# Splitting the first loads of a float32 feature network by partitions over two DMA queues, with seven fewer warm-up matmuls

## The reference

```python
w = jnp.einsum('bpf,mf->bpm', features, W_ft) + b_ft
accumulator = stm * w
l1_x = jnp.clip(accumulator, 0.0, 1.0).reshape(features.shape[0], -1)
l2_x = jnp.clip(l1_x @ W1.T + b1, 0.0, 1.0)
return l2_x @ W2.T + b2
```

## Time and profile before

| | us |
|---|---|
| median of 3 runs | 399.14 |
| lowest and highest of them | 398.35, 399.34 |
| the profiled execution, its own time | 398.15 |
| its span, first to last instruction | 396.4 |
| TensorE matmul busy | 392.8 (99%) |
| VectorE busy | 346.9 (88%) |
| ScalarE busy | 197.6 (50%) |
| HBM read | 96.87 MB, 244 GB/s over the span |

### The profile page before, as it was taken

The page is one execution under the profiler, slowest core; times in us unless marked ns, Lnnn a source line. Parts: engine busy times, 40 slices in busy tenths (PEclk is TensorE's granted clock), DMA queues, the critical chain, the costliest instruction groups (busy, mean ns, idle before and its releaser), DMA issues.

```text
span 396.4 us, 4869 instructions
## 1 busy us (share of the span) xinstructions
PE 392.8 (99%) x1862; PEld 323.7 (82%) x1862; DVE 346.9 (88%) x347; ACT 197.6 (50%) x207; POOL 14.7 (4%) x34
## 2 busy tenths in 40 slices
PE   8999999999999999999999999999999999999997
PEld 6888888888888888888888888888788888878886
DVE  3999999999999999999997789999787754999624
ACT  5565556633484434444334864344433447863500
POOL 0000034041000000000000000000000000000000
PEclk9999999999999999999999999999999999999999
DMA  8999979989976677666607689887667778774000
GB/s 271 394 398 400 383 247 362 342 256 230 327 255 233 237 254 263 243 220 235 233 0 256 225 317 397 327 308 236 203 233 257 241 217 247 245 246 132 0 2 3
DMA packets 30775, 97.85 MB, mean 247 GB/s; under 512 B 4024, under 2 KB 10176, under 8 KB 25312
## 3 DMA queue, kind: packets, MB, share of 16 engines
q1 hardware_dynamic: 29392, 95.18, 69.0%
q0 software_dynamic: 1072, 2.10, 1.7%
q10 hardware_dynamic: 288, 0.26, 0.2%
HBM read 96.87 MB, written 0.00 MB: 244 GB/s over the span
## 4 chain that ended last, share of the span: by engine, by line
PE 99%; DVE 0%; issue 0%; DVEq 0%
PE sums L595 94%; PE sums L672 3%; PE sums L711 1%; PE sums L698 1%; PE sums L688 0%; PE sums L706 0%; DVE res L528 0%; DVE hid L522 0%; DVE idle L531 0%; DVEq L527 0%
## 5 line engine op out<-in xcount | busy, mean ns | idle before, releaser
L595 PE MATMUL sums<-x_hi,w_hi 128*128 128x512 f32 x544 | 167.2, 391 | 0.0
L595 PE MATMUL sums<-x_hi,w_lo 128*128 128x512 f32 x544 | 166.5, 389 | 0.0
L595 PEld LDWEIGHTS sums<-x_hi,w_hi 128*128 128x128 f32 x544 | 102.1, 188 | 21.9 <-issue 0.7
L595 PEld LDWEIGHTS sums<-x_hi,w_lo 128*128 128x128 f32 x544 | 102.4, 188 | 21.3
L595 PE MATMUL sums<-x_lo_home,w_hi 128*128 128x512 f32 x384 | 118.4, 389 | 0.0
L355 ACT ACTIVATE x_hi<-xs 128x2048 fp32r<-128x2048 f32 x58 | 110.7, 1908 | 2.2 <-DVE xs L490 1.8
L350 ACT ACTIVATE w_hi<-ws 128x512 fp32r<-128x512 f32 x58 | 36.9, 636 | 147.1 <-PE sums L595 139.0
L499 DVE TENSOR_TENSOR x_lo_home<-xs,x_hi 128x2048 fp32r<-128x2048 f32 x40 | 91.3, 2283 | 12.3 <-ACT x_hi L355 12.3
L595 PEld LDWEIGHTS sums<-x_lo_home,w_hi 128*128 128x128 f32 x384 | 72.1, 188 | 15.0
L483 DVE TENSOR_TENSOR xs<-xs 128x2048 f32<-128x2048 f32 x20 | 45.6, 2281 | 0.7 <-DMA xs<-x_p 0.7
L496 DVE TENSOR_TENSOR w_lo<-ws,w_hi 128x512 fp32r<-128x512 f32 x58 | 39.6, 683 | 6.2 <-ACT w_hi L350 6.1
(11 more groups left out here) (72 smaller groups left out, 199.5 us busy)
## 6 DMA issues: line engine op xcount, KB each, us to landing
xs<-x_p SPq DMA_DIRECT2D x40, 1024.0 KB, 5.7
xs<-x_p SPq DMA_DIRECT2D x56, 512.0 KB, 6.4
ws<-w_p SPq DMA_DIRECT2D x56, 256.0 KB, 3.5
ws<-w_p SPq DMA_DIRECT2D x44, 128.0 KB, 4.7
open_x<-x_p SPq DMA_DIRECT2D x3, 512.0 KB, 6.2
xr_raw<-x_rest POOLq DMA_DIRECT2D x1, 1024.0 KB, 8.5
stm_all<-stm SPq DMA_DIRECT2D x1, 1024.0 KB, 7.6
open_x<-x_p SPq DMA_DIRECT2D x2, 256.0 KB, 4.3
```

The costliest lines, as they stand in the source:

```text
L595: return nc.tensor.matmul(sums[:, bank, :], w[:, m * P:(m + 1) * P], x[:, c * BANK:(c + 1) * BANK], start=start, stop=stop, skip_group_che ...
```

## The change

A new input, `head`, is laid out on the host: for each of 128 partitions the first 512 columns of X of step 0 and the 256 columns of W of step 0 side by side, 768 float32, 3 KB a partition. It is loaded by two transfers, partitions 0 to 63 on SyncE's queue and 64 to 127 on ScalarE's. The other 512 columns of X of step 0, and X of step 1, are split by partitions over the two queues in the same way. W of step 1 moves from ScalarE's queue to SyncE's, between them. The rounding of the first piece is shared: ScalarE rounds columns 0 to 319 of X (`SHARE`), VectorE rounds W and columns 320 to 511 (`share_hi`). X of step 1 is rounded in two pieces instead of one. Warm-ups go from 22 to 15. Everything from step 2 on is as it was. `highs_before` counts one rounding less than `halves_before`, since W's is no longer ScalarE's.

```diff
+SHARE = 320
-WARM_UP = 22
+WARM_UP = 15
...
+        head_in = sb("head_in", [P, BANK + MH], at=c_at + 4 * (STAGED * COLS - BANK))
...
         def pieces(g, pos):
-            if (g, pos) == (0, 0) or (g < STAGED and pos == 1):
+            if pos == 0 and g < 2 or pos == 1 and g < STAGED:
                 return (0, BANK), (BANK, COLS)
...
+        def open_b11(g, a, b):
+            if g:
+                return open_x[:, STAGED - 1 - g, a:b]
+            return head_in[:, a:b] if b <= BANK else open_x[:, STAGED - 1, a - BANK:b - BANK]
+
+        def open_a11(g):
+            return open_w[:, g, :] if g else head_in[:, BANK:]
...
         def _(sp):
-            sp.dma_start(open_x[:, 0, 0:BANK], x_p[0, :, 0, 0:BANK]).then_inc(open_x_loaded[0], 16)
-            sp.dma_start(open_x[:, 0, BANK:COLS], x_p[0, :, 0, BANK:COLS]).then_inc(open_x_loaded[STAGED], 16)
+            sp.dma_start(head_in[0:P // 2, :], head[0:P // 2, :]).then_inc(head_in_loaded[0], 16)
+            sp.dma_start(open_x[0:P // 2, STAGED - 1, 0:BANK], x_p[0, 0:P // 2, 0, BANK:COLS])\
+                .then_inc(open_x_loaded[0], 16)
+            sp.dma_start(open_w[:, 1, :], w_p[1, :, 0, :]).then_inc(open_w_loaded[1], 16)
...
-                    sp.dma_start(open_x[:, g, :], x_p[g, :, 0, :]).then_inc(open_x_loaded[g], 16)
+                    rows = P // 2 if g == 1 else P
+                    sp.dma_start(open_x[0:rows, STAGED - 1 - g, :], x_p[g, 0:rows, 0, :])\
+                        .then_inc(open_x_loaded[g], 16)
...
-                if pos == 0 and g < STAGED:
+                if (g, pos) == (0, 0):
+                    for j in range(2):
+                        sc.wait_ge(head_in_loaded[j], 16)
+                    nc.scalar.activation(x_hi[:, 0, 0, 0:SHARE], open_b11(0, 0, SHARE), ACT.Copy).then_inc(open_hi, 1)
+                    sc.wait_ge(open_x_loaded[0], 16)
+                    sc.wait_ge(open_x_late[0], 16)
+                    nc.scalar.activation(x_hi[:, 0, 0, BANK:COLS], open_b11(0, BANK, COLS), ACT.Copy)\
+                        .then_inc(open_hi, 1)
+                elif pos == 0 and g < STAGED:
...
-            for g in range(2):
-                sc.dma_start(open_w[:, g, :], w_p[g, :, 0, :]).then_inc(open_w_loaded[g], 16)
+            sc.dma_start(head_in[P // 2:P, :], head[P // 2:P, :]).then_inc(head_in_loaded[1], 16)
+            sc.dma_start(open_x[P // 2:P, STAGED - 1, 0:BANK], x_p[0, P // 2:P, 0, BANK:COLS])\
+                .then_inc(open_x_late[0], 16)
+            sc.dma_start(open_x[P // 2:P, STAGED - 2, :], x_p[1, P // 2:P, 0, :]).then_inc(open_x_late[1], 16)
...
+            for j in range(2):
+                dve.wait_ge(head_in_loaded[j], 16)
+            nc.vector.tensor_copy(w_hi[:, 0, 0, :], open_a11(0)).then_inc(share_hi, 1)
+            nc.vector.tensor_copy(x_hi[:, 0, 0, SHARE:BANK], open_b11(0, SHARE, BANK)).then_inc(share_hi, 1)
...
             def open_products(n, g, pos):
                 before = halves_before(n)
+                rounded = highs_before(n)
...
+                if n == 0:
+                    pe.wait_ge(share_hi, 2)
                 for i, cs in enumerate(groups):
-                    pe.wait_ge(open_hi, before + 2 + i)
+                    pe.wait_ge(open_hi, rounded + 2 + i)
...
+        "head": np.concatenate([x_p[0, :, 0, :BANK], w_p[0, :, 0, :]], axis=1),
```

More of the change, by code:

```diff
@@ L53, in pass_of, with feature_net @@
     return f, g - f * K_PAIRS
-def feature_net(nc, x_p, w_p, x_rest, w_rest, stm, b_ft, w1_t, b1, w2_t, b2, out):
+def feature_net(nc, head, x_p, w_p, x_rest, w_rest, stm, b_ft, w1_t, b1, w2_t, b2, out):
     L1 = w1_t.shape[2]
@@ L132, in feature_net @@
         open_w_loaded = [sem(f"open_w_loaded{j}") for j in range(STAGED)]
-        open_x_loaded = [sem(f"open_x_loaded{j}") for j in range(STAGED + 1)]
+        head_in_loaded = [sem(f"head_in_loaded{j}") for j in range(2)]
+        open_x_late = [sem(f"open_x_late{j}") for j in range(2)]
+        open_x_loaded = [sem(f"open_x_loaded{j}") for j in range(STAGED)]
         open_hi = sem("open_hi")
         open_lo = sem("open_lo")
+        share_hi = sem("share_hi")
         a_done = sem("a_done")
@@ L230, in halves_before, with highs_before @@
             return sum(1 + len(pieces(*half)) for half in OPEN_HALVES[:n])
+        def open_b11(g, a, b):
[4 more added lines that the diff above has]
+            return open_w[:, g, :] if g else head_in[:, BANK:]
+        def highs_before(n):
+            return halves_before(n) - 1
         def x_sums(g):
@@ L317, in open_half @@
                     sc.wait_ge(step_done if pos else a_done, g - HI + 1)
-                if pos == 0 and g < STAGED:
+                if (g, pos) == (0, 0):
[7 more added lines that the diff above has]
+                elif pos == 0 and g < STAGED:
                     sc.wait_ge(open_w_loaded[g], 16)
-                    nc.scalar.activation(w_hi[:, g % HI, 0, :], open_w[:, g, :], ACT.Copy).then_inc(open_hi, 1)
+                    nc.scalar.activation(w_hi[:, g % HI, 0, :], open_a11(g), ACT.Copy).then_inc(open_hi, 1)
                     sc.wait_ge(open_x_loaded[g], 16)
[L322 to L325, removed]
+                    if g == 1:
+                        sc.wait_ge(open_x_late[1], 16)
+                    for a, b in pieces(g, 0):
+                        nc.scalar.activation(x_hi[:, g % HI, 0, a:b], open_b11(g, a, b), ACT.Copy).then_inc(open_hi, 1)
                 elif pos == 0:
@@ L432, in open_low @@
             def open_low(n, g, pos):
-                before = halves_before(n)
+                before = highs_before(n)
                 if pos == 0 and g < STAGED:
-                    w_src, x_src = open_w[:, g, :], open_x[:, g, :]
-                elif pos == 0:
-                    w_src, x_src = ws[:, raw_w(g), :], xs[:, raw_x(g), :]
-                else:
-                    w_src, x_src = ws[:, raw_w(g) + 1, :], xs[:, TST + g, :]
-                dve.wait_ge(open_hi, before + 1)
+                    w_src = open_a11(g)
+                else:
+                    w_src = ws[:, raw_w(g) + pos, :]
+                if n == 0:
+                    dve.wait_ge(share_hi, 1)
+                else:
+                    dve.wait_ge(open_hi, before + 1)
                 nc.vector.tensor_tensor(w_lo[:, slot(g), pos, :], w_src, w_hi[:, g % HI, pos, :].bitcast(F32),
                                         ALU.subtract).then_inc(open_lo, 1)
+                if n == 0:
+                    dve.wait_ge(share_hi, 2)
                 for i, (a, b) in enumerate(pieces(g, pos)):
                     dve.wait_ge(open_hi, before + 2 + i)
-                    nc.vector.tensor_tensor(low_x(g)[:, pos, a:b], x_src[:, a:b],
+                    if pos == 0 and g < STAGED:
+                        x_src = open_b11(g, a, b)
+                    else:
+                        x_src = xs[:, TST + g if pos else raw_x(g), a:b]
+                    nc.vector.tensor_tensor(low_x(g)[:, pos, a:b], x_src,
                                             x_hi[:, g % HI, pos, a:b].bitcast(F32), ALU.subtract)\
@@ L454, in sums_of @@
                 if f == 0:
-                    if staged:
+                    if 0 < g < STAGED:
                         dve.wait_ge(open_w_loaded[g], 16)
@@ L462, in sums_of @@
                         dve.wait_ge(open_x_loaded[g], 16)
-                        if g == 0:
-                            dve.wait_ge(open_x_loaded[STAGED], 16)
+                        if g < 2:
+                            dve.wait_ge(open_x_late[g], 16)
                     else:
                         dve.wait_ge(x_loaded[n], x_count(g))
-                    b11 = open_x[:, g, :] if staged else xs[:, j, :]
                     for a, b in pieces(g, 1):
-                        nc.vector.tensor_tensor(xs[:, TST + k, a:b], xs[:, TST + k, a:b], b11[:, a:b],
-                                                ALU.subtract).then_inc(x_sum, 1)
+                        b11 = open_b11(g, a, b) if staged else xs[:, j, a:b]
+                        nc.vector.tensor_tensor(xs[:, TST + k, a:b], xs[:, TST + k, a:b], b11, ALU.subtract).then_inc(x_sum, 1)
                     if k >= LATE_S2:
```

## The result

| | before | after |
|---|---|---|
| median of 16 runs each | 398.35 | 400.17 |
| lowest and highest | 397.59, 399.34 | 398.74, 402.32 |
| the profiled execution, its own time | 398.15 | 401.79 |
| its span | 396.4 | 399.9 |

The ratio of after to before is 1.0051, with a 95% interval of 1.0036 to 1.0066: slower by 0.5%, more than the 0.3% that the prediction set as its bound. The forecast was 399.3 with no measurable change; its range held the result. The medians of this table differ by 1.82, and of the four cases the first rival (the clock rises later), at +1.7, comes nearest to that. The profiled execution lies 1.6 us above its kernel's median, so it shows the mechanism at more than its median size.

A forecast was written before the change was run, and what follows sets the result against it. The prediction took TensorE's first-product start and product pace as the bound. The later start gave +0.2, other terms +0 and +0; added to 399.14, the profiled execution corrected to the median, this made 399.3, range 398.2 to 401.5.

The forecast's parts named there:

- the first rival: TensorE idle ahead of the first product makes its clock rise later: +1.0 to +2.5, middle +1.7, 400.8; chance 0.38.
- The likeliest case: First product near 5.9 and the clock's rise as before: 398.9 to 399.7, all within 0.3%; chance 0.40.
- What bounds the kernel: TensorE's unbroken matmuls: only the first real product's start and the products' pace can move the end.
- The landing of the head: Opening transfer of X's first piece and W of step 0: lands at 4.1, between 3.4 and 4.84.
- The table load behind the landing: ScalarE's 1.28 us ACT_TABLE_LOAD waits for the head; first product at 5.94 instead of 5.61, worth +0.2 us.
- VectorE's casts: Rounding of W and X's 192 columns on VectorE: done by 4.9, hidden under the table load.
- I take the rise as unmoved, at 7.05: +0.: Seven warm-ups less leave TensorE idle about 1.6 us before the products, yet its clock rises at 7.05: +0.
- The bytes come when they came: SyncE's transfers issue one slot, some 0.45 us, later, but the DMA backlog keeps landings unchanged: price 0.
- All three covers hold: X's second piece, X of step 1 and VectorE's later remainders stay in time for TensorE: price of each 0.
- The table load is not in the way: Rival at the start: VectorE's casts decide, first product at 4.25 to 4.95; 398.4 to 398.8; chance 0.10.
- the halves land no earlier: Rival at the head: landing stays at 4.84, start at 6.68; +0.6, 399.7, more if the clock rises later; chance 0.12.

The follow-up runs named there:

- run 4: run 1 with each split load as one 128-partition transfer and W of step 1 back on ScalarE's queue, 15 warm-ups; 398.86, ratio to before 1.0002.
- run 5: run 4 with 22 warm-ups instead of 15; 397.53, ratio to the kernel before 0.9979.
- run 6: run 4 with 18 warm-ups instead of 15; 397.89, ratio to the kernel before 0.9985.
- run 9: run 5 without the early ACTIVATE, so the table load again stands behind the head's wait; 399.13, ratio to the kernel before 1.0019.
- run 10: run 5 with W of step 1 as SyncE's third transfer instead of ScalarE's first; 398.44, ratio to the kernel before 1.0004.
- run 8: Kernel before, with the rest of X of step 0 and X of step 1 split by partitions over two queues; 399.76, ratio to before 1.0038.
- run 12: run 1 with 22 warm-ups instead of 15; 399.14, ratio to the kernel before 1.0034.
- run 2: Changed kernel with 26 warm-ups instead of 15; 399.35, ratio to the kernel before 1.0029.
- run 3: Kernel before with 15 warm-ups instead of 22, nothing else; 399.67, ratio to the kernel before 1.0028.
- run 7: run 1 with each of the three split loads cut by columns instead of by partitions; 397.95, ratio to the kernel before 0.9983.
- run 1: Changed kernel with a one-column ACTIVATE ahead of the head's wait, so the table load runs early; 398.93, ratio to the kernel before 1.0019.
- run 11: run 5 with the head alone split by columns over the two queues, 20 warm-ups; 398.02, ratio to the kernel before 0.9997.

## Why the prediction was right or wrong

The forecast of no measurable change was wrong in its mechanism, and the prediction's own list of signs says so: one of them is "if the clock's rise moves", and it moved. That the result lies in the range is luck as far as the forecast's chain goes. The likeliest case alone had 398.9 to 399.7; the range reached 401.5 for the sake of a rival that was given 0.38. The base was off as well: the three runs before had a median of 399.14, the sixteen have 398.35, and with that base the forecast would have been 398.5 and the miss 1.6 us, not 0.9.

**What bounds the kernel.** Right: the start and the pace of products. Nearly all of what was found lies in the first 13 us.

**The landing of the head.** Taken as 4.1, between 3.4 and 4.84. The halves landed 4.0 and 3.2 us after their issue (ScalarE's, SyncE's):

```profile
head_in<-head ACTq DMA_DIRECT2D x1, 192.0 KB, 4.0
head_in<-head SPq DMA_DIRECT2D x1, 192.0 KB, 3.2
```

The later one counts, 4.71, near the upper bound; mis-sized by 0.6 us. In one transfer it came 3.1 to 3.8 us after its issue (runs 4, 5, 6, 9, 10). The Trainium skill's rule (DMA: Bandwidth & Descriptors, section Rules for kernel authors), that splitting by partition halves gains nothing, is borne out by runs 8 and 12; here the split even lost.

**The table load behind the landing.** Right in mechanism and size: 4.79 to 6.07, then the rounding from 6.08; start at 6.66, where 5.94 was forecast, 0.6 of the difference being the landing and 0.1 the small steps between (the sum also took 0.45 for the rounding that it had worked out as 0.47). Run 9 shows it alone. The 1.38 us of drain that the Trainium skill adds (ScalarE: Activation LUTs, section What ACT_TABLE_LOAD costs) did not appear: the ACTIVATE starts 0.01 us behind the load. The page gives it for a switch to a different table set; here the load is the only one in the trace.

**VectorE's casts.** Hidden, as said. They took 0.29 and 0.25 us, the faster of the two cases that were left open:

```profile
4.81 0.29 DVE L570 CAST w_hi<-head_in 128x256 fp32r<-128x256 f32 x1 [3.81 <-DMA head_in<-head]
5.02 0.25 DVE L571 CAST x_hi<-head_in 128x192 fp32r<-128x192 f32 x1
```

**"I take the rise as unmoved, at 7.05: +0."** This is the step that failed, and it decides the sign. The rise went to 12.8. The rival had priced it: 6.0 us behind the first product, that is 6.66 + 6.0 = 12.7. The middle it took, +1.7, is near the 1.82 between the medians; its end, +2.5, is nearer to the profiled run's 3.6, which started 0.7 later still. Runs 2 and 3 show that ending the warm-ups early does it. That its size follows one rule is not shown, as run 3 rose at 10.2, 4.6 behind its first product, so that the 12.7 came out as priced is partly luck. Nor does every gap do it. Of the 14 profiles, one a kernel, only those of the changed kernel and of run 3, with gaps of 2.70 and 1.65 us ahead of the rise, rose later than before; with gaps of 0.31, 0.44, 0.98 and 1.24 us (runs 6, 7, 4, 1) the products were at the upper pace by 6.4. The argument against the rival, that the warm-ups were not shown to count because the clock rose 1.4 us into the products, was weak: one execution does not show when others rise.

**"The bytes come when they came" for X of step 1.** Wrong. Its later half landed at 9.4, not 7.1. Of the 2.3 us, 0.9 are a later issue (2.62 for 1.68), more than the one place in the queue that the prediction allowed for, and 1.4 are a slower transfer (6.8 for 5.4). DMA issues after, at 1.99 and 2.62 us:

```profile
open_w<-w_p SPq DMA_DIRECT2D x1, 128.0 KB, 6.4
...
open_x<-x_p SPq DMA_DIRECT2D x1, 256.0 KB, 6.8
```

The full DMA share was read as a fixed rate; it is not one, see the two stretches above. In the changed kernel this cost nothing, because TensorE at the lower clock needed X of step 1 only at 11.5: one fault covered the other. It is why mending the load or the gap by itself (runs 1 and 2) gave back only part, and why run 12, with both mended, is still 0.34% slower than before.

**"All three covers hold."** No wait showed at any of them: the second piece of X was there when ScalarE was done with the first, and X of step 1 was covered only as just said. The third held too: VectorE's remainder of (4,0) ended at 30.49 and TensorE was later than before, so no wait showed.

**The table load is not in the way; the halves land no earlier.** The first was not the case. The second was nearly so for the head, and much more than so for what followed it.

What stays open: with transfers that reach all 128 partitions, runs 7, 10 and 11 still had X of step 1 about 1 to 2 us later than runs 4, 5, 6 and 9 (8.06 to 8.92 for 6.68 to 7.12), and 226 to 254 GB/s from 5 to 6.5 us for 277 to 342, at a DMA share of 0.68 to 0.87 for 0.89 to 0.98. Neither W's place nor the second queue is common to all three. In all three the head was there before 4 us; whether this matters was not tried.

## What to carry to other kernels

Read the order of instructions for what a compiler-inserted ACT_TABLE_LOAD waits for: a second wait ahead of the first ACTIVATE moved 1.28 us from the shadow of the first transfer onto the path here, and one tiny early ACTIVATE moves it back. Let warm-ups reach the first real product; taken away, they cost 0.28% here by themselves, and the loss varies from run to run. Leave a load whole, or cut it by columns: cut by partitions, the same kernel was 0.36% slower than cut by columns (runs 1 and 7). Mend faults that hide each other together, since one can cover another.

## What the runs showed of the hardware that was not expected

- Transfers to 64 partitions on both queues moved 219 to 261 GB/s at a DMA share of about 1 from 5 to 8 us in the changed kernel, against 387 to 396 in the same stretches before. The Trainium skill (DMA: Bandwidth & Descriptors, section The descriptor swizzle) has each DMA engine write one port of the on-chip memory in a 128-partition transfer; that half the partitions would share fewer ports is an inference that no run here shows.
- Issuing a transfer of 64 partitions was not cheaper: three took 0.57, 0.70 and 0.79 us on ScalarE's sequencer, where two of 128 partitions took 0.87 together before.
- The clock's rise moves from execution to execution even with no gap: 6.0 us behind the first warm-up in the profile of before, about 4.5 in that of run 5, whose warm-ups are the same. In the profile of run 4 it rose within the 15 warm-ups, which took 3.20 us for 3.38 in the changed kernel; that its slower times, 2 us higher, go with later rises is an inference.
